# First cross attention: the temper's second matmul moves behind the next slot's scores and first half of the turning

## The reference, cut to what matters

```python
scores = qk / math.sqrt(dk)
mean_sim = scores.mean(axis=(-2, -1))
max_sim = scores.max(axis=-1).mean(axis=-1)
probs = jax.nn.softmax(scores, axis=-1)
entropy_proxy = jnp.var(probs, axis=-1, ddof=1).mean(axis=-1)
feats = jnp.stack([mean_sim, max_sim, entropy_proxy], axis=-1)
hidden = jax.nn.gelu(_linear(feats, w1, b1), approximate=False)
hidden = jax.nn.gelu(_linear(hidden, w2, b2), approximate=False)
log_t = jnp.clip(_linear(hidden, w3, b3), LOG_T_MIN, LOG_T_MAX)
t = jnp.exp(log_t)[..., None]
attn = jax.nn.softmax(qk / (2.0 * t), axis=-1)
out = jnp.einsum('bhqk,bhkd->bhqd', attn, V)
```

## Time and profile before

| | us |
|---|---|
| median of 3 runs (2054.84 to 2058.22) | 2057.4 |
| the profiled execution | 2057.52 |
| its span in the profile | 2055.5 |
| PE busy in the span | 1695.4 |
| DVE busy | 1273.8 |
| ACT busy | 1203.0 |
| POOL busy | 399.5 |

### The profile page before, as it was taken

How to read it: one execution, slowest core, us unless ns; L and a number is a source line. 1 busy time by engine, 2 the same in 40 slices (tenths; PEclk the granted TensorE clock), 3 DMA queues, 4 the chain that set the end, 5 groups by cost and what they waited for, 6 DMA issues and landing times. The chain is left out here.

```text
span 2055.5 us, 31160 instructions
## 1 busy us (share of the span) xinstructions
PE 1695.4 (82%) x11522; PEld 986.2 (48%) x11522; DVE 1273.8 (62%) x1804; ACT 1203.0 (59%) x2497; POOL 399.5 (19%) x369
## 2 busy tenths in 40 slices
PE   3999999999999446888875748999999995888861
PEld 1444444444434125666653324666666664666651
DVE  0777777777777368777345424666666664566627
ACT  2777877777777326777821525555555553466533
POOL 0111111011011036666400001222222221110000
PEclk9999999999999656888965869999999997899985
DMA  4000000000000000000000010000000000000001
GB/s 118 1 11 1 0 11 0 0 0 0 0 1 0 8 16 4 8 2 1 2 3 0 0 42 1 1 1 1 1 1 1 1 2 13 11 8 5 2 3 41
DMA packets 36377, 16.66 MB, mean 8 GB/s; under 512 B 15286, under 2 KB 35088, under 8 KB 36240
## 3 DMA queue, kind: packets, MB, share of 16 engines
q1 hardware_dynamic: 32080, 8.91, 2.0%
q10 hardware_dynamic: 4160, 5.90, 0.8%
HBM read 12.71 MB, written 2.10 MB: 7 GB/s over the span
## 5 line engine op out<-in xcount | busy, mean ns | idle before, releaser
L1985 POOL TENSOR_TENSOR self_probs<-self_probs,self_rz 128x1024 f32<-128x1024 f32 x64 | 121.3, 1895 | 548.6 <-DVE self_rz L2013 548.6
L1960 ACT ACTIVATE self_probs<-self_scores,self_neg 128x128 f32<-128x128 f32 x512 | 181.4, 384 | 16.7 <-DVE self_neg L2008 16.7
L525 POOL TENSOR_SCALAR gru_decay<-gru_zgate 128x512 f32<-128x512 f32 x96 | 75.5, 787 | 591.7 <-ACT gru_zgate L478 566.4
L389 PE MATMUL gru_gate<-gru_xn,gru_whg 128*128 128x512 f32 x384 | 182.6, 598 | 3.5 <-DVE gru_xn L568 3.5
L393 PE MATMUL gru_hid<-gru_xn,gru_whg 128*128 128x512 f32 x384 | 181.4, 595 | 0.0
L401 PE MATMUL gru_out<-gru_y,gru_wo 128*128 128x512 f32 x384 | 178.1, 599 | 0.7 <-DVE gru_y L596 0.7
L1016 PE MATMUL x_turned<-const_ident,x_probs 128*77 128x128 f32 x1024 | 156.8, 302 | 11.5 <-ACT x_pt L1118 9.4
L1118 ACT ACTIVATE x_pt<-x_turned 77x512 f32<-77x512 f32 x224 | 122.3, 583 | 64.7 <-PE x_turned L1016 64.4
L1016 PEld LDWEIGHTS x_turned<-const_ident,x_probs 128*77 128x77 f32 x1024 | 128.3, 163 | 61.7 <-issue 28.5
L1210 DVE TENSOR_REDUCE x_m<-x_scores 128x16 f32<-128x1232 f32 x64 | 92.0, 1437 | 94.3 <-PE x_scores L1005 94.1
L591 DVE SCALAR_TENSOR_TENSOR gru_ghid<-gru_hid,gru_half_c,gru_sighid 128x512 f32<-128x512 f32 x96 | 71.8, 747 | 114.6 <-ACT gru_sighid L479 114.5
(11 more groups left out here) (347 smaller groups left out, 3550.3 us busy)
## 6 DMA issues: line engine op xcount, KB each, us to landing
gru_whg<-in_L_attn_Whg ACTq DMA_DIRECT2D x4, 768.0 KB, 10.1
x_ctx_in<-in_ctx SPq DMA_DIRECT2D x16, 154.0 KB
gru_xin<-in_x SPq DMA_DIRECT2D x8, 256.0 KB, 2.9
out<-moe_res SPq DMA_DIRECT2D x8, 256.0 KB, 2.3
gru_wo<-in_L_attn_Wo ACTq DMA_DIRECT2D x4, 384.0 KB, 11.0
self_w_raw<-in_L_attn_Wq SPq DMA_DIRECT2D x1, 512.0 KB, 6.0
self_w_raw<-in_L_attn_Wk ACTq DMA_DIRECT2D x1, 512.0 KB, 6.7
self_w_raw<-in_L_attn_Wv SPq DMA_DIRECT2D x1, 512.0 KB, 9.1
```

The source lines that it names most:

```text
L389: mm(ps_gate[n % 2][:, :], whg[:, l, k, DI + c * P:DI + (c + 1) * P], xn[u][:, k, :], start=(k == 0), stop=(k == KH - 1))
L1960: last = f(probs[n % 2][:, a, jj, :], ps_s[n % 2][:, a, jj * T:(jj + 1) * T], ACT.Exp, bias=neg[n % 2][:, a, jj:jj + 1], accum_out=z[n % 2 ...
L1985: pool.tensor_tensor(probs[n % 2][:, :, :, :], probs[n % 2][:, :, :, :], whole, ALU.mult).then_inc(pn_ready.sem, 1)
```

## The change

The table `PLACES` gives t1 alone the second place of slot `r` = 1, and t2 with t3 the first place of slot `r` = 2. The function `place` returns for the pair, when it is asked for the matmuls, the whole chain t2, its reader, t3, its reader, and nothing when it is asked for the readers. The number of instructions is the same on every engine; the order in which the one `misc` bank is used is the same too.

```diff
         if temper:
-            PLACES = [(("context", 1), ("keys", 1)), (("queries", 1), ("t12", -1)), (("t3", -1), ("values", 1)), (("mix", -3), ("var", -3))]
+            PLACES = [(("context", 1), ("keys", 1)), (("queries", 1), ("t1", -1)), (("t23", -1), ("values", 1)), (("mix", -3), ("var", -3))]
         else:
...
             if at_ is None or not 0 <= n // GB + at_[1] < NG:
                 return []
-            kinds = ("t1", "t2") if at_[0] == "t12" else (at_[0],)
-            return [(kind + "_out" * read, n // GB + at_[1], 0) for kind in kinds]
+
+            if at_[0] == "t23":
+                return [] if read else [(kind, n // GB + at_[1], 0) for kind in ("t2", "t2_out", "t3", "t3_out")]
+            return [(at_[0] + "_out" * read, n // GB + at_[1], 0)]
```

## The result

The changed kernel took 2032.9 us, median of 4 runs (2029.2 to 2038.3), against 2057.4 before (4 runs by then): a ratio of 0.9885 (0.9861 to 0.9909). The profiled execution took 2033.31, its span 2031.6 against 2055.5, so 23.9 us are to be found.

What follows compares the result with a forecast made beforehand. It took a once-a-group cycle of waits in the first cross attention, no engine full, as the bound; 10.0 + 2.5 + 0.7 = 13.2 us off 2057.5 gave 2044.3 us, bounds 2041.9 to 2046.8, range 2038 to 2052.

Steps and rivals of the forecast that it cites:

- The links: Slot 2 of a temper group: start times forecast link by link for scores, turnings, t3, attend and values' copy.
- the middle between the two ends of the clock: Gain per group at attend in slot 2: 1.66 us, taken between 1.36 and 1.96.
- the upper end: Second turning of slot 2 at full clock: attend at 838.6, a gain of 1.96 us a group.
- six groups: Second to seventh temper: six times 1.66, 10.0 us gained.
- the rival of the other slow stretch: Var's half clock also goes in five groups: 5 x 0.94 = 4.7 us more gained, 2039.6 us; chance 0.15.
- The main sum: First cross attention: 10.0 + 2.5 + 0.7 = 13.2 us gained, bounds 10.7 and 15.6; chance 0.55.
- the last temper: Last temper, turnings but no scores behind it: copies ahead of the table load gain 0.7 us, bounds 0 and 1.34.
- first temper: First temper, in the filling without turnings: DVE's idle 2.48 before its maximum goes, 2.5 us gained.
- the lower end: Second turning of slot 2 at half clock: attend at 839.2, a gain of 1.36 us a group.
- Half clock all through slot 2: PE in slot 2 stays at half clock: 0.35 us gained a group, 2052 us; chance 0.09.
- given back: The cycle closes through an unmoved POOL or ACT link: only the first temper's 2.5 us stays, 2055 us; chance 0.06.
- the reload: Copies between the two Gelus load their own table, two more ACT loads of 1.28: 4.5 us slower, 2062 us; chance 0.04.

Runs made afterwards that it cites:

- after_filled: Changed kernel plus two unused matmuls (512 and 128 columns) ahead of attend in slot 3; 2033.6 us, ratio 0.9895.
- before_filled: Kernel before plus two unused matmuls (512 and 384 columns) between t1 and t2, scores still behind t2; 2048.6 us, ratio 0.9963.
- before_longer: Kernel before plus one unused DVE reduction of about 1.0 us in slot 0 of groups from the fourth on; 2072.8 us, one run.
- after_longer: Changed kernel plus one unused DVE reduction of 3.95 us in slot 0 of groups from the fourth on; 2088.2 us, one run.
- alternate: Changed kernel with the change kept in groups 2, 4 and 6 alone, t2 ahead of the scores in the others; 2044.5 us, ratio 0.9951.
- t2_behind_scores: Half of the move against the kernel before: t2 behind slot 2's scores but ahead of its first turning, t3 at its old place; 2051.3 us, ratio 0.9982.
- clip_filled: Changed kernel with t3 behind the second turning, its clip between DVE's sums, and unused matmuls (512 and 128 columns) in slot 3; 2025.3 us, ratio 0.9847.

## Why the prediction was short

**The links were right.** Every place that the prediction names came within 0.3 us of it, counted from t1's last pair: scores 0.32 (0.33 forecast), t3 3.82 (3.83), second turning 4.06 (4.2), attend 5.04 (5.3 at full clock), values' copy 8.06 (8.3). The wait before t3 is 1.04, that before t2 0.2, DVE's before the maximum of slot 2 1.05, and there are still 8 loads at each of the two Gelus' places (the 26 loads that the prediction counts in all are in no profile; both have 160). Two of its signs failed. DVE's wait before the values' copy stayed at 0.48, where 0.5 to 1.1 was named, and a clean group takes 30.0 us and not 34.0, where 1.4 to 2.0 less was named: 2.3 of the 4.0 lie between slots 1 and 3, 1.55 at var.

**First step that failed: the middle between the two ends of the clock.** I took 1.66 a group, between attend at half clock (1.36) and at full clock (1.96), since half of the pause was left. In the change's three profiles the second turning of slot 2 took 1.05 in all 18 groups, so the upper end stood. It was itself 0.24 short, by two links that I had taken long: t3 to turning 0.24 (0.35), turning to attend 0.98 (1.1). 1 to 2 and 2 to 3 together gained 13.1 in six groups, 2.18 each, where 1.66 stood: 3.1 us missing. One may divide these 13.1 with the filled kernel of before: 10.6 are order at equal clock, 2.5 the half clock gone. The choice would have asked for a reason why a pause of 1.04 should do half of what one of 1.98 does; I had none but the ratio. A half clock did follow such a pause once, in after_filled, and cost 2.8 us, but in none of the change's 18 groups.

**Second: the rival of the other slow stretch.** It was priced at 0.94, the difference of var alone. The stretch covers the scores behind var too, which DVE waits for: 1.55 (9.37 and 7.82). The earlier trace rows show both, scores at 1.41 right behind var. And it isn't all or nothing. The prediction counts five vars at half clock; there are four. Before, five slots with `r` = 3 have a slow stretch (turnings of 1.99 at 820.68, 854.53, 888.46 and two more); four of them hold a var, the one of group 2 falls behind attend, where it cost some 0.4 (6.46, and 6.10 in after_filled, which had none). After the change three vars were spared in each of three profiles, 3 x 1.55 = 4.7, while group 2's stretch came earlier and fell on its attend, which took 1.94: its 3 to 0 is 8.41 and no longer 6.46. So the sum of 3 to 0 fell by 2.7 (3.1 between the second profiles), and 0 to 1 by 0.8 in the same groups. The main sum held this at nothing and the rival had 0.15; that the place of a stretch can move was to be seen in group 7, whose var was spared before (1.10 at 985.76). Why three of four were spared after the change is not shown.

**Third: what hangs on the clock elsewhere.** In the drain the last output projection ran at half clock in both profiles of before and at full clock in all three of the change:

```profile
1035.02 2.05 PE L1050 MATMUL x_misc<-x_oT,x_w_o 128*128 128x512 f32 x2 [1.59 <-DVE x_oT L1248]
```

```profile
1014.99 1.10 PE L1052 MATMUL x_misc<-x_oT,x_w_o 128*128 128x512 f32 x2 [1.59 <-DVE x_oT L1250]
```

It is alone on the path there, so its 0.95 counts whole. But the place of t2 does not decide it: with t2 where it was, it took 1.10 in before_filled and in before_longer, and with the whole change it took 1.74 in after_filled. The drain's other 0.8 is the last temper, as the 0.7 forecast: from its table load to the next slot's turning 7.51 before (997.28 to 1004.79) and 6.71 after (978.05 to 984.76). The later stages gave 2.9 in this pair of profiles; PE is busy 816.6 us there for the same 7033 matmuls that took 819.8 before, which looks like the clock, though its mean reads 0.88 in both. The prediction names that as what would make it wrong, but its range held nothing for it.

**The sum, again**, with the forecast in brackets: first temper 2.6 (2.5), six groups 13.1 (10.0), last temper 0.8 (0.7): 16.5 (13.2), and with it 2.7 and 0.8 in the slots between, 1.0 in the drain and 2.9 behind the stage: 23.9. At equal clock the order alone is worth 2.6 + 10.6 + 0.8, about 14. That the forecast's 13.2 stands near it is luck: its own value for the order at an equal clock was the lower end, 1.36 a group, 8.2 in six where 10.6 came, and half of the clock's gain filled most of the difference. Of the other 10 us, 2.5 are the half clock behind the pause, shown by filling it; 3.5 in the slots between and 1.0 in the drain stand at rows with the other clock, but what moved it is open; the 2.9 behind the stage did not come again.

**The rivals.** Half clock all through slot 2, given back and the reload did not come. On the reload: the Trainium skill, "ScalarE: Activation LUTs", section "Table sets: the hidden batching unit", says that Relu is in every set, and the trace agrees; the two copies between the two Gelus take 1.08 together, with no load of their own. On the clock, the rows show a pause before t2 (1.98 in ten groups, 2.34 and 2.23 in the first of each profile) and 0.50 behind it in all twelve groups of the two profiles of before, and 1.00 at the turning where it was filled (6 of 6). The Trainium skill, "TensorE: Matmul & The Clock Gate", section "HAM oscillation — how this bites in real kernels", by which such a pause does no harm, would leave 2 to 3 at some 8.3 in before_filled; it measured 7.82. The same page of the Trainium skill, section "A second HAM failure mode: psum-queue depth-cycling", tells of frequent small pauses between groups of matmuls that make the clock swing; the traces here agree with that one, with pauses of 1.0 to 2.0 us.

## What stays open

Which group the slow stretch at var falls into. It hit groups 3 to 6 in both profiles of before, and of these in the changed kernel group 5 once and group 4 twice; it left group 5 out when only the pause before t2 was filled, and group 4 under a pad of 1.0 us. That the period or the pauses ahead of it decide is argued, not shown; the run meant for it (after_longer) made pauses of its own. Nor is it known why one pause of 1.98 in `alternate`, and those of group 4 in `t2_behind_scores`, were harmless, and what moves the later stages by 3 us. A pause of PE of 1.61 before attend stands ahead of var in groups 3 to 6 of both kernels. Filling it left no var at half clock in the slots of after_filled and clip_filled, but with one profile each, and with a new slow stretch elsewhere in each, that is a hint and not proof.

## What to carry to other kernels

When PE waits for a chain through another engine, put work behind which nothing of that chain stands into the wait, all that is ready and not just the first piece: the scores alone cured DVE's stall and the time came back one step later. A pause of 1 to 2 us on PE can have a second price, the half clock on what follows, which is to be read from what that work feeds. In this kernel it was 0.5 us on a turning, 1.55 on var with scores behind it, 2.8 on attend, 3.7 on turning, attend and values in a row. So price a change of the clock over every instruction that the slow stretch covers, and where the trace shows the clock at both levels, keep both whole ends in the range.

## What was not expected of the hardware

- A clock of 0.50 behind PE pauses of 1.98 to 2.34 us (12 of 12 groups of before, 2 of 3 in `alternate`), behind pauses of 1.25 to 1.51 and 1.34 (4 of 6 groups of t2_behind_scores), and once behind 1.04 (after_filled), where the same pause was harmless in the 18 groups of the change. Pauses of 1.24 and 1.34 at the last temper of the kernel before were harmless too (turning 1.15).
- Unused matmuls of 32 columns' output, 512 and 384 long, kept the clock at 1.00 at the turnings of all six groups: 8.6 us in the medians of the whole kernel, of which the profile of the stage shows 4.5.
- The same kernel puts its slow stretches in different groups from execution to execution, and runs of one kernel lay 6 to 9 us apart (2031.2 to 2037.4, 2029.2 to 2038.3).
- An extra 3.95 us on DVE once a group cost 6 to 11 us a group, with pauses on PE and a clock of 0.51 in the slot behind them.
